# A fused attention and mixture-of-experts layer: the output projection of tile i-2 moves behind the weighted values of tile i, and its add to the end of VectorE's step

## The reference, cut to what matters

```
sq, sk = elu1(q), elu1(k)                     # 16 heads of 16 channels
coarse = (sq @ M) / clip(sq . z)              # a memory shared by all tokens
fine   = sum over 4 banks of w * (sq @ M_n) / clip(sq . z_n)
gprob  = sigmoid(relu(coarse @ w1.T + b1) @ w2.T + b2)
memory = gprob * fine + (1 - gprob) * coarse
local  = causal linear attention, in chunks   # scores, running state S and z, division
out    = gate * memory + (1 - gate) * local
x      = x + out @ w_o.T + experts(xn)
```

## Time and profile before

| | |
|---|---|
| median of 3 runs | 646.67 us (643.94 to 651.8) |
| profiled execution | 644.98 us |
| its span | 643.2 us, mean granted TensorE clock 0.964 |
| busy share of the span | PE 90%, weight loads 76%, DVE 74%, ACT 53%, POOL 49% |
| chain that ended last | PE 28%, DVE 6%, issue 5%, ACT 2%; its costliest line is L1467 with 4% |

### The profile page before, as it was taken

The page is one execution under the profiler, slowest core; times in us unless marked ns, Lnnn a source line. Parts: engine busy times, 40 slices in busy tenths (PEclk is TensorE's granted clock), DMA queues, the critical chain, the costliest instruction groups (busy, mean ns, idle before and its releaser), DMA issues. The chain is left out here.

```text
span 643.2 us, 21856 instructions
## 1 busy us (share of the span) xinstructions
PE 576.3 (90%) x7929; PEld 491.8 (76%) x7929; DVE 476.2 (74%) x1254; ACT 343.2 (53%) x791; POOL 317.7 (49%) x392
## 2 busy tenths in 40 slices
PE   1998999998999599999999969889989998899995
PEld 0786887886888499999999947667767777677773
DVE  3484485484488387777777776979987997889995
ACT  4547648638646244334344435656656665566653
POOL 2047047057055473111010013878886887788885
PEclk9999999999999699999999976989999998999998
DMA  9034734725437343764444442354282426342220
GB/s 311 35 114 171 248 124 186 246 105 199 167 142 282 99 126 126 234 210 140 138 147 131 130 139 71 105 134 137 66 275 62 150 81 233 92 143 85 77 69 34
DMA packets 65036, 92.66 MB, mean 144 GB/s; under 512 B 9556, under 2 KB 49460, under 8 KB 64948
## 3 DMA queue, kind: packets, MB, share of 16 engines
q1 hardware_dynamic: 54644, 69.76, 32.7%
q0 software_dynamic: 8032, 21.12, 10.7%
q10 hardware_dynamic: 2272, 0.53, 0.4%
HBM read 51.13 MB, written 40.24 MB: 142 GB/s over the span
## 5 line engine op out<-in xcount | busy, mean ns | idle before, releaser
L1724 POOL DMA_INDIRECT yg<-d_grouped_y,from_row x64 | 80.4, 1256 | 15.1 <-issue 10.7
L995 ACT ACTIVATE silu<-e_up 128x176 f32<-128x176 f32 x72 | 22.9, 318 | 90.3 <-PE e_up L91 90.3
L1551 ACT ACTIVATE with_mem<-a_ring 128x680 f32<-128x680 f32 (+2 forms) x63 | 46.7, 742 | 19.1 <-PE a_ring L1432 19.1
L89 PE MATMUL e_up<-wb,xb 128*128 x144 | 50.9, 354 | 1.4 <-DVE xb L1018 1.4
L833 POOL TENSOR_TENSOR ticks<-lane 128x1 f32<-128x1 f32 x4 | 2.3, 563 | 92.8 <-DVE slot_i L746 92.8
L91 PE MATMUL e_up<-wb,xb 128*128 x144 | 46.9, 325 | 0.0
L90 PE MATMUL e_up<-wb,xb 128*128 x144 | 46.8, 325 | 0.0
L1575 ACT ACTIVATE attT<-a_ring 128x256 f32<-128x256 f32 x32 | 12.3, 384 | 64.1 <-PE a_ring L1461 64.1
L1672 DVE TENSOR_TENSOR probs<-a_ring,causal_s 128x1024 f32<-128x1024 f32 (+3 forms) x46 | 39.8, 892 | 4.0 <-PE a_ring L1452 3.8
L1032 DVE TENSOR_TENSOR h_sb<-e_up,silu 128x128 f32<-128x128 f32 x72 | 21.0, 292 | 28.3 <-ACT silu L995 20.3
L667 DVE TENSOR_TENSOR silu<-t_u,silu 128x512 f32<-128x512 f32 (+1 forms) x24 | 16.4, 685 | 32.6 <-PE t_u L91 13.5
(11 more groups left out here) (284 smaller groups left out, 2031.8 us busy)
## 6 DMA issues: line engine op xcount, KB each, us to landing
v<-d_rows SPq DMA_DIRECT2D x77, 128.0 KB, 2.1
d_grouped_y<-y_sb SPq DMA_DIRECT2D x73, 128.0 KB, 1.9
d_v<-v_half SPq DMA_DIRECT2D x8, 544.0 KB, 4.1
d_q<-halves SPq DMA_DIRECT2D x8, 512.0 KB, 3.1
d_k<-halves SPq DMA_DIRECT2D x8, 512.0 KB, 3.2
total<-d_base SPq DMA_DIRECT2D x8, 512.0 KB, 4.5
out<-total SPq DMA_DIRECT2D x7, 512.0 KB
v<-d_v SPq DMA_DIRECT2D x6, 544.0 KB, 6.8
```

The source lines that it names most:

```text
L89: pe.matmul(out, a[0], b[0], start=start, stop=False)
L1551: act.activation(with_mem[n % 3][:, :, :].rearrange("p (m q) w -> p q m w", m=KC)[:, lo:hi, :, 0:WN], ring[:, at:at + hi - lo, 0:KC * WN]. ...
L1724: pool.indirect_dma_start(yg[tile % GATHERS][:, k, :], None, d["grouped_y"], bass.IndirectOffsetOnAxis(ap=c["from"][:, k, tile:tile + 1], ...
```

## The change

`oproj` moves in two of the three lists. On TensorE, step i now has `oproj` of tile i-2 between `values` and the second `state` of tile i, in place of `oproj` of tile i-3 between `scores` and `outT`. On VectorE, the add of `oproj` stands at the end of step i, behind `norms` of tile i+1, and is of tile i-2; before it stood behind `scores` and was of tile i-3. ScalarE's list stays. No instruction is added or taken away; the ring still has 15 items in a step, in a new order, so that items take other banks and wait for other readers.

```
 def tensor_order():
-    for i in range(len(TILES) + 3):
-        here = i < len(TILES)
+    for i in range(len(TILES) + 2):
+        here, behind = i < len(TILES), 0 <= i - 2 < len(TILES)
         if here:
             order += [("scores", *TILES[i], j) for j in range(PP)]
-        if 0 <= i - 3 < len(TILES):
-            order.append(("oproj", *TILES[i - 3], 0))
-        if 0 <= i - 2 < len(TILES):
+        if behind:
             order.append(("outT", *TILES[i - 2], 0))
         if not here:
+            order.append(("oproj", *TILES[i - 2], 0))
             continue
...
         order += [("values", b, t, j) for j in range(2)]
+        if behind:
+            order.append(("oproj", *TILES[i - 2], 0))
         if t < NT - 1:
             order.append(("state", b, t, 1))
         order.append(("local", b, t, 0))
...
 def vector_order():
...
         order += [("local", *TILES[i - 1], 0), ("scores", *TILES[i], 0)]
-        if i > 2:
-            order.append(("oproj", *TILES[i - 3], 0))
         order += [("coef", *TILES[i - 1], 0), ("rest", *TILES[i - 1], 0), ("fine", *TILES[i - 1], 0)]
         if i + 1 < len(TILES):
             order.append(("norms", *TILES[i + 1], 0))
+        if i >= 2:
+            order.append(("oproj", *TILES[i - 2], 0))
...
-    return order + [("oproj", *tile, 0) for tile in TILES[-3:]]
+    return order + [("oproj", *tile, 0) for tile in TILES[-2:]]
```

## The result

The changed kernel takes 676.27 us in the median of four runs (674.87 to 679.12), the kernel before 647.6 beside it: 1.0484 times as long, interval 1.0435 to 1.0534. That is slower by 29 us where 658 with a range of 646 to 668 was forecast. The size of the undisturbed step was as worked out; what the steps lose beyond it was not. The chances had put no clear change (0.57) ahead of slower (0.39).

A forecast was written before the change was run, and what follows sets the result against it. The prediction took a loop of VectorE and POOL, 7.29 us a step, as the bound. 9.0 - 1.3 + 4.2 = +11.9 on 644.98 gave 656.9; with the median 1.7 above, about 658, range 646 to 668.

The forecast's parts named there:

- no clear change: The whole kernel's time within two per cent of the kernel before; chance 0.57, against 0.39 for slower.
- The loop: Attention step: division, mask, norms, values, `oproj`, `local`, next division, each awaiting the last; 7.58 us against 7.29, +9.0 in all.
- 0.3 was to be saved: Steps whose fourth bank of scores is masked apart: norms needs only the first three; 0.3 in 4 steps, -1.3.
- Stalls lose their cover: TensorE's issue stalls in the attention phase, with slow clock behind two, cost 17.0 against 12.8: +4.2, ends 0 and +8.
- 0.81 of slack: TensorE's `local` ends 0.81 us before the division needing it in the kernel before, swallowing part of each stall.
- the +11.9 of the sum: Whole kernel: 9.0 - 1.3 + 4.2 us, added to the profiled execution's 644.98, gives 656.9.
- Rival 1: TensorE's waits for the mask beside stalls drop its clock: 18 us more, 676; chance 0.13.
- Rival 2: By the weight-load rule VectorE is the bound; VectorE and POOL keep the step at 7.29, 645 to 647; chance 0.14.
- VectorE's cost of 0: Moving VectorE's add behind `coarse` costs 0, its waits being covered; without cover 0.41 a step, 13 in all.
- The other covers: VectorE's moved add: `oproj` and POOL's sum are done before `coarse` ends, and the next division waits for later matmuls anyway.
- The ring's new partners: `turned`, `local` and scores wait for other readers of their banks; costed at nothing, 0.26 if the gate's bank is late.
- the ends 650 and 668: Whole kernel's time with both ends of the step loop and of the stalls, from 644.98.

The follow-up runs named there:

- E1: The changed kernel with the second of the two matmuls of each output projection left out behind values: 656.89 us (1.0147).
- E2: The changed kernel with one unused matmul added in each step at the old place, between scores and `outT`: 668.56 us (1.0353).
- E4: The kernel before, order untouched, with two unused matmuls (1.06 us) added ahead of `local` in each step: 665.51 us (1.0296).
- E5: The changed kernel with 32 unused matmul calls at the program's start: 677.43 us (1.0513).
- E6: The changed kernel with 48 unused matmul calls at the program's start: 667.95 us (1.034).
- E11: The changed kernel with 16 unused matmul calls at the program's start: 662.47 us (1.0245).
- E16: The changed kernel with 40 unused matmul calls at the program's start: 666.06 us (1.0304).
- E7: The kernel before with 32 unused matmul calls at the program's start: 661.89 us (1.0261).
- E9: The kernel before with 48 unused matmul calls at the program's start: 674.66 us (1.0442).
- E10: The kernel before with 16 unused matmul calls at the program's start: 664.64 us (1.032).
- E15: The kernel before with 40 unused matmul calls at the program's start: 659.75 us (1.0201).
- E12: The changed kernel's TensorE list, but VectorE's add back behind the mask, of tile i-3: 691.74 us (1.0749).

## Why the prediction was wrong

**The loop: right.** 7.58 was worked out, 7.61 to 7.65 came, and 7.38 where 0.3 was to be saved. The timeline shows it, with norms behind the mask and the division 0.03 behind `local`, and E1 and E2 bear it out: less behind norms makes the step shorter, more ahead of norms does not make it longer. E4 adds nothing to this, since TensorE has no idle time left in it. The steps together cost 10, where 7.7 had been put.

**Stalls lose their cover (+4.2, ends 0 and +8): this step failed.** It measured +23, with 19 us of stalls and 40 us of the phase at the lower clock, 14 before. It took the stalls of the kernel before as given in number, place and length, and let only their cover change. E5, E6, E11 and E16 hold the new order and lose 17 to 26 above their undisturbed steps; E7, E9, E10 and E15 hold the old order and lose 18 to 33. So the loss is no less with 0.81 of slack than without (24 in the mean of five places, 23 in the new order). The kernel before stands at the best of five places for its order (13), the changed one at the worst of five for its own (37). So the mean leaves no lost cover to pay for, and the change's own cost in it is its step, as far as five places tell. That the +11.9 of the sum is near the 9.5 is luck: 4.2 of it did not come, and the step cost 2 more. By this mean some 24 of the 33.5 come from where the boundaries of TensorE's code fall, 11 from the old order's good place and 13 from the new one's bad place. That the place decides is shown by the shifts and by the return at 64 calls; the 24 is an estimate from five places.

What TensorE waits for can be read from the list of transfers, which has a queue for code (packets, MB, share of 16 engines; changed kernel):

```profile
q8 instruction: 66, 1.08, 0.7%
```

These are 66 transfers of 16384 bytes, for 17039 instructions of TensorE, one for each 256 or so. In the phases of the 18 traces TensorE passes 799 boundaries, never earlier than 1.1 us after such a transfer has landed, and the 219 stalls at them of 0.3 us or more end 1.1 to 1.9 us after it, 1.4 in the median. For the stall that ends at 500.00 the transfer ran from 497.05 to 498.68. A boundary stalls when its transfer started late: of 117 that started less than 1 us behind the boundary ahead, one stalled, of 213 that started 3 us or more behind it, 143. Why a transfer starts late is open. Other transfers at the time seem to matter (half of the boundaries stalled where the DMA engines had been busy for over 0.6 of the 2 us before the transfer's start, 18% elsewhere), and so does TensorE's pace (E12), but no run took either alone.

**Rival 1, the clock: a near number, another cause.** It gave 676 and had low clock behind the stalls, which came: 0.93 in the phase. The sign set for it, more stretches of low clock, came too. But it charged the short waits for the mask. In E16 norms waits for the mask in 29 steps, 0.6 in the mean, and the clock is 0.97, as in the kernel before:

```profile
405.28:657.85 252.57, 224.00 (x5537) 172.29 (x5522) 222.19 (x417) 144.78 (x341) 190.90 (x212) 0.97 0.37 112
```

The low clock follows the stalls, in either order: but for the first steps (the phase begins at the lower clock in all traces), each of the 72 stretches at 0.50 in the 18 traces came behind a stall of 1.0 us or more. The prediction cited the Trainium skill, "TensorE: Matmul & The Clock Gate", section "A second HAM failure mode: psum-queue depth-cycling", for short waits at PSUM banks; it is not borne out by the waits here.

**Rival 2, the rule of weight loads of the Trainium skill, "Perfetto Trace Analysis", section "Identifying the Most-Contended Engine": wrong here.** Weight loads fell to 66% (180.59 of 272.31), and VectorE is busy 80% of the phase; no engine became fuller while the step grew. A loop through two engines sets it.

**VectorE's cost of 0: wrong by 0.2 a step, hidden.** E1 shows it: `coef_c` against POOL's addition. So the move made two chains longer, TensorE's to 7.61 to 7.65 and VectorE's to 7.49 to 7.55; without the first the second would still have cost 0.2 a step, some 7 us. The other covers held, but for the add, which waits when TensorE stalls within values.

**The ring's new partners at nothing: right.** The wait for the gate's bank shows once, 1.3 us, as before; E12 shows what `turned` would have cost with the add left where it was.

**Two slips of the sum.** 656.9 + 1.7 is 658.6, not 658, and the ends 650 and 668 leave the 1.7 out; neither changes the account.

## What to carry to other kernels

Work that fills one engine's wait for another is free there and dear anywhere inside the loop that both share: before a move, mark which wait it fills, then add a little load at the old place and take a little from the new one (E2, E1). Adding the whole load (E4) can fill the engine and then says nothing of the place. A timing of one order against another in a long unrolled program includes where the boundaries of the code blocks fall; here that alone was worth 20 us in either order. Before a change of a few per cent is believed, either way, move the code by several parts of a block and time both orders at each.

## What the runs showed of the hardware that was not expected

TensorE's stalls without a releaser lie on a grid of 125 matmuls with their weight loads, and 64 extra calls (128 matmuls and as many loads) bring them back to the same matmuls. Of the 228 in the phases of the 18 traces (0.3 us or more), 219 stand at the same place of the grid, 193 to 196 instructions past a multiple of 256 from TensorE's first, whatever the order, and they end 1.1 to 1.9 us after 16384 bytes of code have landed. The Trainium skill, "Runtime: NRT & Kernel Launch", section "Instruction fetch mechanics", says that code is refilled in blocks of 256 instructions and that fetching is mostly hidden; the trace agrees on the 256 and not on the hiding, with 8 to 24 us of stalls in 31 steps. At the program's start, where TensorE mostly waits, the calls were not free either: 32 of them ran for 13.9 us, where TensorE's first work had come at 12.3, and 64 for 27.6. With 32 the first division came at 402 or 403 us, with 64 at 413 or 414, against 395. And a VectorE instruction on 128x16 elements, 0.23 us alone, took 0.41 in the median of the changed kernel, where it mostly met POOL's addition.
